# Chunk 0's first layer and first layer-2 group in two halves of 256 columns, the picks in front, and another order on ScalarE and on the sync engine

## What is computed

```python
for (W, b), split in zip(conv_params, split_flags):        # W1 (128, 1024), W2 and W3 (128, 2048)
    z = jnp.einsum('bhd,bmd->bhmd', x, x0).reshape(B, h * x0.shape[1], D)
    xk = jax.nn.relu(jnp.einsum('oc,bcd->bod', W, z) + b[None, :, None])
    if split:                                              # layers 1 and 2
        x, xk = (xk[:, :half], xk[:, half:])
    results.append(xk)
return jnp.sum(jnp.concatenate(results, axis=1), axis=2) @ Wo.T + bo
```

## Time and profile before

| | before |
|---|---|
| median of 3 runs | 461.61 us |
| the profiled execution's own time | 461.44 us |
| its span, first to last instruction | 459.4 us |
| mean granted clock of PE | 0.992 |
| PE busy | 447.3 us (97%) |
| DVE busy | 418.3 us (91%) |
| POOL busy | 394.2 us (86%) |
| ACT busy | 309.6 us (67%) |
| DMA | 75.66 MB, mean 165 GB/s |

### The profile page before, as it was taken

How to read it: one execution, slowest core, us unless ns; L and a number is a source line. 1 busy time by engine, 2 the same in 40 slices (tenths; PEclk the granted TensorE clock), 3 DMA queues, 4 the chain that set the end, 5 groups by cost and what they waited for, 6 DMA issues and landing times.

```text
span 459.4 us, 6013 instructions
## 1 busy us (share of the span) xinstructions
PE 447.3 (97%) x1602; PEld 299.0 (65%) x1602; DVE 418.3 (91%) x481; ACT 309.6 (67%) x389; POOL 394.2 (86%) x145
## 2 busy tenths in 40 slices
PE   7899599999999999999999999999999999999997
PEld 2344376667777676776767677676777767677774
DVE  3677589999999999999999999999999999999997
ACT  3752477868687685867758587775858768586661
POOL 0070388999989898998989899898989989999995
PEclk8999899999999999999999999999999999999999
DMA  7999987998959779595977959597694943822100
GB/s 277 236 225 220 228 176 171 216 218 190 223 126 222 156 166 223 114 228 120 221 161 164 224 112 228 116 226 163 158 229 102 239 103 78 190 46 48 33 12 0
DMA packets 22943, 75.66 MB, mean 165 GB/s; under 512 B 5779, under 2 KB 5907, under 8 KB 18836
## 3 DMA queue, kind: packets, MB, share of 16 engines
q1 hardware_dynamic: 22932, 75.52, 74.7%
HBM read 59.51 MB, written 0.00 MB: 130 GB/s over the span
## 4 chain that ended last, share of the span: by engine, by line
PE 92%; DMA 4%; ACT 1%; DVE 1%; issue 1%; SPq 1%; DVEq 0%; ACTq 0%
PE y_ps L854 28%; PE y_ps L842 16%; PE y_ps L844 16%; PE y_ps L860 16%; PE y_ps L850 7%; PE y_ps L818 4%; PE y_ps L866 4%; DMA a_rep<-x_sb 3%; DMA shifted<-x_dram 1%; DVE z L653 1%; PE y_ps L846 1%; PE y_ps L862 1%; SPq L364 0%; ACT results L475 0%; ACT x_sb L465 0%
## 5 line engine op out<-in xcount | busy, mean ns | idle before, releaser
L610 POOL TENSOR_TENSOR zl<-z,zh 128x1024 fp32r<-128x1024 f32 (+1 forms) x135 | 386.3, 2897 | 38.3 <-ACT zh L514 38.3
L653 DVE TENSOR_TENSOR z<-a_ps,b_fac 128x512 f32<-128x512 f32 (+2 forms) x256 | 273.4, 1092 | 21.5 <-PE y_ps L866 10.9
L514 ACT ACTIVATE zh<-z 128x1024 fp32r<-128x1024 f32 (+1 forms) x135 | 168.8, 1250 | 112.6 <-DVE z L653 112.1
L860 PE MATMUL y_ps<-zl,w_high 128*128 128x512 f32 x315 | 146.5, 557 | 0.0
L842 PE MATMUL y_ps<-zh,w_high 128*128 128x512 f32 x315 | 124.7, 396 | 4.7 <-ACT zh L514 4.7
L844 PE MATMUL y_ps<-zh,w_low 128*128 128x512 f32 x315 | 123.4, 392 | 0.0
L854 PE MATMUL y_ps<-z,w_raw 128*128 128x512 f32 x240 | 122.3, 591 | 0.0
L860 PEld LDWEIGHTS y_ps<-zl,w_high 128*128 128x128 f32 x315 | 59.0, 188 | 64.3 <-issue 56.3
L842 PEld LDWEIGHTS y_ps<-zh,w_high 128*128 128x128 f32 x315 | 59.2, 188 | 18.8 <-issue 5.7
L844 PEld LDWEIGHTS y_ps<-zh,w_low 128*128 128x128 f32 x315 | 59.4, 189 | 13.3 <-issue 0.2
L854 PEld LDWEIGHTS y_ps<-z,w_raw 128*128 128x128 f32 x240 | 45.1, 188 | 9.9
(11 more groups left out here) (55 smaller groups left out, 205.6 us busy)
## 6 DMA issues: line engine op xcount, KB each, us to landing
b_fac<-xt_dram SPq DMA_DIRECT2D x52, 512.0 KB, 8.7
shifted<-xt_dram SPq DMA_DIRECT2D x60, 256.0 KB, 4.9
a_rep<-x_sb SPq DMA_DIRECT2D x91, 128.0 KB, 2.6
shifted<-xt_dram SPq DMA_DIRECT2D x60, 128.0 KB, 5.1
b_fac<-xt_dram SPq DMA_DIRECT2D x16, 256.0 KB, 8.3
a_rep<-x_sb SPq DMA_DIRECT2D x62, 64.0 KB, 2.1
w_raw<-w_dram SPq DMA_DIRECT2D x2, 640.0 KB, 8.2
shifted<-x_dram SPq DMA_DIRECT2D x2, 512.0 KB, 5.5
```

Source lines behind the costliest of these rows:

```text
L514: nc.scalar.activation(zh[:, slot, 0:end - native, :], z[:, slot, native:end, :], ACT.Copy).then_inc(zh_ready, 1)
L610: nc.gpsimd.tensor_tensor(zl[:, slot, 0:end - native, :], z[:, slot, native:end, :], zh[:, slot, 0:end - native, :].bitcast(F32), ALU.subtract
L653: return nc.vector.tensor_tensor(dst, factor.unsqueeze(1).to_broadcast(list(dst.shape)), others, ALU.mult)
L860: mm = nc.tensor.matmul(y, wh[layer][:, w, :], zl[:, slot, t, :], start=False, stop=end_here)
```

## The change

It does four things.

- All eight picks stand ahead of layer 1: the second four get banks of their own (`pick_banks[1]`), ACT copies all eight out before it rounds layer 1's weights, and three float32 matmuls of 256 columns on zeros (`WARM`) follow them on PE.
- Layer 1 of chunk 0 (`first_layer`) is added up in two halves of 256 columns, the first in `y_ps[1]`, the second in `y_ps[3]`. DVE makes the first tile's product alone, then the weight sum, then the second tile. The first half signals `y0_half_done` three half-matmuls before the end.
- Group q=1 (`first_product`) is made and used in halves: ACT copies the first half of `a_ps`, DVE copies the second half from the bank itself, and each half's products are two instructions of 2 x 256 columns. ACT writes layer 1's outputs in halves too (`first_results`).
- The order on ACT in iteration 2 and on SP is another one: layer 1's output of chunk 1 moves ahead of `a_to_psum(3, 1, 0)`, each `x_to_psum` moves ahead of the `a_to_psum` that it stood behind, and SP issues `spread(1, 1)` ahead of `load_b_half(2, 0)`. As SP waits for all eight picks before it loads layer 3's weights (`load_w(3, ...)`), that load comes earlier as well.

```diff
@@ sync engine
             load_b_half(1, 1)
+            spread(1, 1)
             load_b_half(2, 0)
-            spread(1, 1)
             load_b_half(2, 1)
             load_x(3)
@@ ScalarE
-            def first_a():
-                act.wait_ge(group_used, 1)
+            def first_results():
+                act.wait_ge(y0_half_done, 1)
                 act.wait_ge(cols_loaded, 16)
+                act.wait_ge(b0_made, 2 * GT)
+                x, early = X_HALF[1], columns[0]
                 for to in (0, HALF):
-                    copy = nc.scalar.activation(a_ps[to:to + HALF, 0, :], y_ps[1][X_HALF[1], :], ACT.Relu,
-                                                bias=cols_sb[X_HALF[1], 0:1])
-                copy.then_inc(a_in_psum[2][0], 1)
+                    copy = nc.scalar.activation(a_ps[to:to + HALF, 0, early], y_ps[1][x, early], ACT.Relu,
+                                                bias=cols_sb[x, 0:1])
+                copy.then_inc(a0_half_in_psum, 1)
+                for n, bank0 in zip(columns, y0_banks):
+                    if n is not early:
+                        act.wait_ge(a_in_psum[2][0], 1)
+                    last_x = nc.scalar.activation(x_out[1][x, n], bank0[x, n], ACT.Relu, bias=cols_sb[x, 0:1])
...
             b_from_psum(0)
+            b_from_psum(1)
...
                     if i_is(i, 2):
+                        if pos == 5:
+                            x_to_sbuf(1, 1)
+                            results_to_sbuf(2, 0)
+                            results_to_sbuf(1, 1)
                         if pos == 6:
                             a_to_psum(3, 1, 0)
-                            results_to_sbuf(2, 0)
-                            y_to_sbuf(1, 1)
                         if pos == 7:
                             act.wait_ge(z_ready, groups_before(2) + 2)
+                            x_to_psum(2)
                             a_to_psum(2, 0, 1)
-                            x_to_psum(2)
...
                         if pos == 4:
+                            x_to_psum(3)
                             a_to_psum(2, 0, 2)
-                            x_to_psum(3)
@@ VectorE
+            def first_product(slot, others, factor):
+                for n, bank0, done in ((columns[0], None, (z1_half_ready, z1_half_ready)),
+                                       (columns[1], y0_banks[1], (z_native_ready, z_ready))):
+                    if bank0 is None:
+                        dve.wait_ge(a0_half_in_psum, 1)
+                    else:
+                        dve.wait_ge(group_used, 1)
+                        x = X_HALF[1]
+                        for to in (0, HALF):
+                            copy = nc.vector.tensor_scalar(a_ps[to:to + HALF, 0, n], bank0[x, n], cols_sb[x, 0:1], 0.0,
+                                                           ALU.add, ALU.max)
+                        copy.then_inc(a_in_psum[2][0], 1)
+                    for t, signal in zip((0, NATIVE_CUT), done):
...
+                        multiply(z[:, slot, t:t + NATIVE_CUT, n], factor[:, n], others[:, t:t + NATIVE_CUT, n]
+                                 ).then_inc(signal, 1)
@@ TensorE
+            def first_layer(weights, tiles):
+                pe.wait_ge(w1_summed, 1)
+                for t in range(NATIVE_CUT):
+                    pe.wait_ge(*((z_native_ready, 1) if t == 0 else (z_second_ready, 1)))
+                    nc.tensor.matmul(y_ps[1][:, columns[0]], weights[t], tiles[:, t, columns[0]],
+                                     start=(t == 0), stop=False)
+                pe.wait_ge(b0_made, GT)
+                for t in range(NATIVE_CUT):
+                    nc.tensor.matmul(y_ps[3][:, columns[1]], weights[t], tiles[:, t, columns[1]],
+                                     start=(t == 0), stop=False)
...
+                for n, bank0 in zip(columns, y0_banks):
+                    for t in range(NATIVE_CUT, GT):
+                        nc.tensor.matmul(bank0[:, n], weights[t], tiles[:, t, n], start=False, stop=False)
+                    pe.wait_ge(z_fifth_ready, 1)
+                    mm = nc.tensor.matmul(bank0[:, n], wq_raw[:, 1, :], z_fifth[:, n], start=False, stop=True)
+                    if n is columns[0]:
+                        mm.then_inc(y0_half_done, 1)
...
             pick_b(0)
+            pick_b(1)
+            for _ in range(WARM):
+                nc.tensor.matmul(y_ps[1][:, 0:2 * P], pooled3[:, 0:P], pooled3[:, 0:2 * P], start=True, stop=True)
             def body(i):
-                if i_is(i, 1):
-                    pick_b(1)
```

More of the change, by code:

```diff
@@ L83 @@
 LOOP = (4, NCHUNK - 2)
+WARM = 3
 LAYERS = {1: (2, 1, 3), 2: (3, 1, 2)}
@@ L281, in cin_kernel @@
         b0_made = sem("b0_made")
+        y0_half_done = sem("y0_half_done")
+        a0_half_in_psum = sem("a0_half_in_psum")
+        z1_half_ready = sem("z1_half_ready")
         b_half_loaded = {c: (sem(f"b{c}_loaded"), sem(f"b{c}_rest_loaded")) for c in range(1, HALVED)}
@@ L289, in cin_kernel @@
         z_native_ready = sem("z_native_ready")
+        z_second_ready = sem("z_second_ready")
         z_ready = sem("z_ready")
@@ L295, in cin_kernel @@
         zxl_ready = sem("zxl_ready")
-        pick_banks = (zx_ps[:, 0, :], zx_ps[:, 1, :], x_ps[:], y_ps[3][:])
+        pick_banks = ((zx_ps[:, 0, :], zx_ps[:, 1, :], x_ps[:], y_ps[3][:]),
+                      (a_ps[:, 0, :], a_ps[:, 1, :], y_ps[2][:], zx_ps[:, 0, :]))
+        columns = (slice(0, CH // 2), slice(CH // 2, CH))
+        y0_banks = (y_ps[1], y_ps[3])
         z_fifth_ready = sem("z_fifth_ready")
@@ L445, in a_to_psum @@
                                      ).then_inc(a_in_psum[layer][half], 1)
-            def first_a():
-                act.wait_ge(group_used, 1)
+            def first_results():
+                act.wait_ge(y0_half_done, 1)
                 act.wait_ge(cols_loaded, 16)
+                act.wait_ge(b0_made, 2 * GT)
+                x, early = X_HALF[1], columns[0]
                 for to in (0, HALF):
-                    copy = nc.scalar.activation(a_ps[to:to + HALF, 0, :], y_ps[1][X_HALF[1], :], ACT.Relu,
-                                                bias=cols_sb[X_HALF[1], 0:1])
-                copy.then_inc(a_in_psum[2][0], 1)
+                    copy = nc.scalar.activation(a_ps[to:to + HALF, 0, early], y_ps[1][x, early], ACT.Relu,
[5 more added lines that the diff above has]
+                    last_x = nc.scalar.activation(x_out[1][x, n], bank0[x, n], ACT.Relu, bias=cols_sb[x, 0:1])
+                    rows = RESULTS[1]
+                    last = nc.scalar.activation(results12[rows, n], bank0[rows, n], ACT.Relu,
+                                                bias=cols_sb[rows, 0:1])
+                last_x.then_inc(x_ready[1], 1)
+                last.then_inc(results_ready[1], 1)
             def x_to_sbuf(layer, c):
@@ L488, in b_from_psum @@
                     act.wait_ge(b0_picked, j + 1)
-                    nc.scalar.activation(b_fac[:, j * CH:(j + 1) * CH], pick_banks[j % GT], ACT.Copy
+                    nc.scalar.activation(b_fac[:, j * CH:(j + 1) * CH], pick_banks[half][j % GT], ACT.Copy
                                          ).then_inc(b0_made, 1)
@@ L654, in multiply @@
                                                ALU.mult)
+            def first_product(slot, others, factor):
[11 more added lines that the diff above has]
+                    for t, signal in zip((0, NATIVE_CUT), done):
+                        if bank0 is not None and t == 0:
+                            dve.wait_ge(a_in_psum[2][0], 1)
+                        multiply(z[:, slot, t:t + NATIVE_CUT, n], factor[:, n], others[:, t:t + NATIVE_CUT, n]
+                                 ).then_inc(signal, 1)
             def product(i, step, k):
@@ L681, in product @@
                     factor = a_ps[:, half, :]
+                    if i_is(c, 0) and layer == 2 and g == 0:
+                        first_product(slot, others, factor)
+                        return
                     dve.wait_ge(a_in_psum[layer][half], c + 1)
@@ L686, in product @@
                 if is_native(q):
-                    multiply(z[:, slot, 0:NATIVE_CUT, :], factor, others[:, 0:NATIVE_CUT, :]
-                             ).then_inc(z_native_ready, 1)
+                    first = 1 if i_is(i, 0) else NATIVE_CUT
+                    multiply(z[:, slot, 0:first, :], factor, others[:, 0:first, :]).then_inc(z_native_ready, 1)
                     if i_is(i, 0):
@@ L693, in product @@
                                                 w1_sb[:, NAT1:2 * NAT1, :], ALU.add).then_inc(w1_summed, 1)
+                        multiply(z[:, slot, first:NATIVE_CUT, :], factor, others[:, first:NATIVE_CUT, :]
+                                 ).then_inc(z_second_ready, 1)
                         dve.wait_ge(x0_loaded[1], 16)
@@ L781, in pick_b @@
                 for r in range(GT):
-                    if half:
-                        pe.wait_ge(b0_made, r + 1)
```

(24 more changed lines are left out.)

8 lines of the change are left out of this document (4 added, 4 removed).

## The result

| | before | after |
|---|---|---|
| median, same chip, 15 runs each | 461.61 us | 459.7 us |
| time over before | | 0.9938 (0.9921 to 0.9954) |
| profiled execution | 461.44 us | 459.70 us, span 457.9 |
| mean granted clock | 0.992 | 0.996 |

By the ratio the change makes the kernel 0.62% faster; the medians lie 1.91 us, 0.41%, apart. Both are under 1%, and the ratio's interval leaves 1 out. One run of the changed kernel, at 928.91 us, is an outlier and is left out of the ratio. The forecast was 457.9 us, range 454.8 to 460.4.

The account below looks back on a forecast made before the run. Start-up transfers on a full DMA were taken to hold up PE, busy 447.3 of 459.4 us. 461.44 - 3.66 (earlier end of layer 2, chunk 2) + 0.15 (given back in layer 3) = 457.9 us, range 454.8 to 460.4.

Parts of the forecast that it names:

- The halves are swallowed: Layer 2 of chunk 0 starts at 13.5 us, not 17.34, but waiting for the spread before q=8 leaves no end effect.
- the mark: End of layer 2 of chunk 2, at 85.48 us before, forecast at 81.82, 3.66 us sooner.
- The order removes the 4.65 us gap: Before layer 1 of chunk 2: the spread lands near 44.9 us, so PE goes on at 47.3 without the gap.
- x3 sets the mark: Layer 1 of chunk 3 waits for x3; layer 2 of chunk 2 ends 19.38 us after `x_ps` is ready.
- x3's landing: Last x3 transfer, issued some 5 us sooner, still lands at 61.84 us because the bytes ahead are the same.
- The rest: After layer 2 of chunk 2: 375.96 us as before, plus 0.15 us given back in the layer 3 behind it.
- the loop never gets its lead back: Rival, chance 0.05: PE waits 0.6 us for POOL in each of 13 iterations, 7.8 us, giving 465.7 us.
- at half clock throughout: Slow case of the front, layer 1 wholly at half clock: layer 2 of chunk 0 ends 1.5 us later.
- The rival of the weights' load: Chance 0.10: layer 3's weights, loaded early, delay x1, x2 and x3 by up to 4.5 us; 460.2 to 462.4 us.
- the useless order: Rival, chance 0.06: the spread before layer 1 of chunk 2 still lands at 49.6 us; 1.8 us gained, 459.6 us.
- x3 sooner: Rival, chance 0.18: x3 lands before 58.9 us, DVE's start of q=10 bounds instead, and the time is 454.7 us.
- the clock stays up in the gap before q=8: Layer 3 of chunk 0: a gap of about 1.8 us before its third group leaves PE's clock up.

Follow-up runs that it names:

- 1: Kernel before with only the new order on ACT and SP, no halves, picks in front or warm-up: 459.23 us, ratio 0.9927.
- 2: Changed kernel with the old order on ACT and SP, so the halves alone: 462.85 us, ratio 1.0011.
- 8: Changed kernel, unaltered, profiled once more: 458.95 us.
- 3: Changed kernel with layer 3's weights loaded only after the wait for layer 1's first output: 459.94 us, ratio 0.9954.
- 4: Changed kernel with x3 issued ahead of chunk 2's two halves of b_fac (2 MB): 457.88 us, ratio 0.9907.
- 7: Kernel before, unaltered, profiled once more: 461.44 us.
- 5: Changed kernel, halves included, with SP's loads and spreads in the order in which they are due: 463.16 us, ratio 1.0027.
- 9: As 5, with halves, but bulk loads cut and put between spreads and one ACT copy an iteration later: 455.65 us, ratio 0.9848.
- 10: Same order of SP and ACT as 9, without halves, picks in front and warm-up: 457.89 us, ratio 0.9899.

## Why the prediction was right, and by how much it missed

- **The halves are swallowed** before the mark: right, and shown by 1 and 2. Layer 2 of chunk 0 starts at 14.58 (forecast 13.5, at most 14), and q=8 waits for the spread. That landed at 40.0 and not at 38.26, so q=8 came at 42.04 instead of 40.3. Some 0.85 us of it go with x1, which landed at 23.20 in place of 22.35; the rest isn't settled.
- **The order removes the 4.65 us gap**: right. `x_ps` of chunk 2 was ready at 40.57 + 0.58 (forecast 39.5), the spread's copy ran at 45.53 (forecast landing 44.9). PE went on at 50.27 and not 47.3, of which 1.74 us come from q=8, and some 3.5 x (1 - 0.59) = 1.4 us from the clock.
- **x3 sets the mark**: right. The step from the start of the copy of x3 to the mark, 0.58 + 19.38 = 19.96 us by forecast, is 83.56 - 63.59 = 19.97 in the changed kernel, 83.23 - 63.23 = 20.00 in 8, and 20.00 in 1 and in 3. So the late q=8 and the clock lost behind its gap cost nothing in the end: in 8, where the clock stayed up, layer 1 of chunk 3 waits longer (1.35 instead of 0.60) and the mark differs only as x3 does. The other runs bear it out: of the changed kernel's fourteen, five have a mean clock of 0.996 and nine of 0.999 or 1.0, and their mean times are 459.36 and 459.34 us. In part that was luck. PE reached layer 1 of chunk 3 at 66.68 - 0.60 = 66.08 us, later than the 64.9 at which the forecast has it start, and x3's own lateness hid that. 4 bounds the rule: with x3 at 54.06 the mark moves by 1.82 us only, and the next spread sets it.
- **The mis-sized term is x3's landing**: 61.84 assumed, 63.57 measured, 1.7 us, which is the whole difference between 457.9 and the 459.70 of the profiled execution. That the landing keeps its time while the issue moves by 5 us was the right direction, but I took it from one execution, and a low one: the kernel before lands x3 at 62.55 in 7. In seven profiles with x3 last in the list x3 lands 39.5 to 40.4 us behind x1, and x1 between 22.35 and 23.8. Of the 1.7 us, some 0.8 are x1's and 0.9 arise between x1 and x3. The twelve profiles on record say more of the first: x1 lands at 22.0 to 23.0 in the five without the halves and at 22.7 to 25.1 in the seven with them, 1.1 us later on the mean, and late too with layer 3's weights held back (3). The forecast had the halves touch no transfer. This points to a delay that comes with them; how isn't shown.
- **The rest** is as forecast: 376.14 us behind the mark, against 376.11, so the rival in which the loop never gets its lead back fell. Some ends in the prediction are loose and change nothing: 457.9 with 1.5 us either way is 456.4 to 459.4 and not 456 to 459.3, and the 1.5 us later "at half clock throughout" aren't worked out. The rival of the weights' load fell by 3; the useless order by 1. x3 sooner didn't come about: the loads moved at 201 to 236 GB/s in the stretches shown. 4 gives that rival a price: 457.88 instead of the 454.7 worked out, since the next spread was late in x3's place.
- **Wrong:** that the clock stays up in the gap before q=8. It did at 1.90 us in 8, and fell at 2.50 us in the profile of the changed kernel. The gap was longer than forecast (1.8), but that is not all: in 1 the clock fell behind 1.75 us, the very gap that had left it up in the earlier trace rows. And the earlier trace rows has a gap of 1.99 us whose next records ran at the lower clock, which the forecast noted and did not set beside the 1.75. By the Trainium skill (TensorE: Matmul & The Clock Gate, Part 1) the clock falls after an idle window, from which I had read that gaps this short leave it up. The traces differ from that, and they decide.

## What to carry to other kernels

Where the DMA is full in a start-up, compute that comes sooner gains nothing until the transfer behind it comes sooner too: ask for each gain which landing ends it, and take that landing from several executions, not one. Reordering a full queue moves the wait to whatever is now behind the bulk (4, 5), and where SP waits for an output, the queue should hold bulk to carry meanwhile (9 against 5: 7.5 us, with two other changes in it). What was worthless beside one bound can pay once that bound is gone, as the halves did between 10 and 9, by their times.

## What the runs showed of the hardware

- Landings differ by more than 1 us between executions of similar kernels, under the same order: x1 at 22.4 and 22.6 us in two of the kernel before, at 22.0 to 25.1 over all twelve profiles, with the same transfers ahead of it. What is queued behind it shifts along (x3 39.5 to 40.4 us later in seven).
- With the DMA full, 1 MB issued 5.7 us later lands 0.4 us later (3).
- A DMA share of 1.0 is not one rate. In the kernel before, 8 to 12 us (weights and `x0`) moved 382 to 386 GB/s at shares of 0.99 and 1.07, and 16 to 22 us (x1 and layer 3's weights) 214 GB/s at 1.03.
- The length of an idle gap alone did not say which clock PE has behind it. It kept 2.4 GHz over 1.75 us in the kernel before (1.00 over the next 3.5 us) and 1.90 us in 8. It had 1.2 GHz for a time behind the same 1.75 us in 1 (0.58 over the next 3.5 us), behind 1.99 us in the kernel before (0.55 over the next 3.7 us), behind 2.50 us (0.59 over 3.5 us) and behind 4.63 us in 5 (0.50 over 4 us).
